# Moving eight more turned tiles of each batch from TensorE's barrier to GpSimd's mask, with a new slot table

## Time and profile before

| | |
|---|---|
| median of 3 runs | 874.0 us (873.55 to 875.01) |
| the profiled execution | 872.33 us |
| its span | 870.6 us |
| TensorE busy (matmul) | 94% |
| VectorE, ScalarE, GpSimd busy | 77%, 63%, 61% |

### The profile page before, as it was taken

The page is one execution under the profiler, slowest core; times in us unless marked ns, Lnnn a source line. Parts: engine busy times, 40 slices in busy tenths (PEclk is TensorE's granted clock), DMA queues, the critical chain, the costliest instruction groups (busy, mean ns, idle before and its releaser), DMA issues.

```text
span 870.6 us, 15444 instructions
## 1 busy us (share of the span) xinstructions
PE 814.5 (94%) x4860; PEld 467.4 (54%) x4860; DVE 674.6 (77%) x1950; ACT 544.3 (63%) x1230; POOL 532.0 (61%) x701
## 2 busy tenths in 40 slices
PE   3869899999999999999999999999999999999986
PEld 2223245646564655656565564656556565646466
DVE  5666669798887969788796978878797888878266
ACT  5427485765758485665848566574957657474832
POOL 4266766675857567585756658575665757474611
PEclk9899899999999999999999999999999999999999
DMA  3350505032140503113050402304050221300000
GB/s 94 100 138 3 141 1 141 1 102 53 43 111 1 152 2 114 41 58 96 5 148 2 141 13 78 76 22 132 2 153 2 85 69 36 106 2 13 13 1 25
DMA packets 49840, 54.75 MB, mean 63 GB/s; under 512 B 7264, under 2 KB 43616, under 8 KB 49760
## 3 DMA queue, kind: packets, MB, share of 16 engines
q1 hardware_dynamic: 49760, 53.76, 22.5%
HBM read 30.28 MB, written 23.07 MB: 61 GB/s over the span
## 4 chain that ended last, share of the span: by engine, by line
PE 54%; DVE 16%; POOL 11%; issue 7%; ACT 6%; DMA 3%; SPq 2%; POOLq 0%; DVEq 0%; ACTq 0%
PE adj L722 12%; PE pv L708 9%; PE score L680 7%; PE turned L694 7%; DVE scrap L955 6%; PE adj L717 6%; PE work L740 4%; PE turned L693 4%; POOL probs_t L547 3%; DVE adj_cos L974 3%; DVE adj_rbf L988 3%; DVE rbf_arg L983 2%; PE work L717 2%; POOL v_cos L632 2%; POOL v_cos L629 2%
## 5 line engine op out<-in xcount | busy, mean ns | idle before, releaser
L547 POOL TENSOR_TENSOR probs_t<-probs_t,keep_t 128x512 int32<-128x512 int32 x256 | 322.4, 1280 | 213.4 <-ACT probs_t L1126 213.1
L955 DVE CUSTOM_DVE_ANT_0 scrap<-score,mask_add 128x512 f32<-128x512 f32 x512 | 340.0, 683 | 67.6 <-PE score L680 65.3
L1126 ACT ACTIVATE probs_t<-turned 128x512 f32<-128x512 f32 x512 | 296.2, 601 | 110.5 <-PE turned L694 105.1
L680 PE MATMUL score<-qk_rows 96*128 96x512 bf16 x512 | 198.9, 388 | 12.1 <-DMA qk_rows<-k_dram 6.0
L694 PE MATMUL turned<-qk_rows 99*128 99x512 bf16 x512 | 196.2, 383 | 9.7 <-ACT probs_t L1126 8.8
L708 PE MATMUL pv<-probs_t,v_cols 128*32 128x512 f32 x1024 | 138.1, 612 | 0.0
L680 PEld LDWEIGHTS score<-qk_rows 96*128 96x128 bf16 x512 | 49.9, 98 | 119.8 <-DVE neg_max L955 55.2
L693 PE MATMUL turned<-bar_t,ident_b 128*128 128x512 bf16 x256 | 98.0, 383 | 0.7 <-ACT probs_t L1126 0.7
L694 PEld LDWEIGHTS turned<-qk_rows 99*128 99x128 bf16 x512 | 50.6, 99 | 54.7 <-ACT probs_t L1126 18.3
L1160 ACT ACTIVATE rbf_exp<-rbf_arg,rbf_bias 128x512 f32<-128x512 f32 x64 | 46.2, 722 | 34.7 <-DVE rbf_arg L983 32.8
L722 PEld LDWEIGHTS adj<-v_cos,adj_cos 128*128 128x128 f32 x480 | 62.8, 191 | 8.8 <-DVE out_sb L1011 0.6
(11 more groups left out here) (159 smaller groups left out, 1221.9 us busy)
## 6 DMA issues: line engine op xcount, KB each, us to landing
q_dram<-split SPq DMA_DIRECT2D x96, 128.0 KB
qk_rows<-q_dram SPq DMA_DIRECT2D x32, 384.0 KB, 4.3
k_dram<-split SPq DMA_DIRECT2D x48, 128.0 KB
qk_rows<-k_dram SPq DMA_DIRECT2D x32, 192.0 KB, 4.8
x_sb<-in_x_dram SPq DMA_DIRECT2D x16, 256.0 KB, 4.2
qk_rows<-k_dram SPq DMA_DIRECT2D x32, 128.0 KB, 4.9
out_dram<-out_sb SPq DMA_DIRECT2D x15, 256.0 KB, 2.5
qk_rows<-k_dram SPq DMA_DIRECT2D x32, 64.0 KB, 5.2
```

The source lines that it names most:

```text
L547: pool.tensor_tensor(tile, tile, keep_t[:, w // HG % T, :], ALU.mult).then_inc(probs_masked.sem, 1)
L680: pe.matmul(score_bank[u % 2][:, :], qk_rows[0:ROWS, b % 2, 0, h, t * P:(t + 1) * P], qk_rows[0:ROWS, b % 2, 1, h, :], start=True, stop=Tr ...
L955: dve.tensor_tensor_reduce(scrap[:, u % 2, :], score_bank[u % 2][:, :], mask_add[:, u % T, :], -1.0, 3.0e38, ALU.add, ALU.min, neg_max[:, ...
L1126: act.activation(probs_t[:, k % 4, w % HG, :], turned_bank[w % 2][:, :], ACT.Exp, scale=SCALE).then_inc(probs_ready.sem, 1)
```

## The change

`MASK_BY_PE` goes from `(2, 3)` to `(3,)`: 8 instead of 16 of a batch's turned tiles get the barrier, and GpSimd masks 24 instead of 16. Stages of all engines get new slots; `AT_BEFORE_LAST` and `AT_LAST` stay as they are. Nothing else is touched.

```diff
-MASK_BY_PE = (2, 3)
+MASK_BY_PE = (3,)
...
-    "hT": (-26,), "q": (-24,), "k": (-22,), "v": (-13,), "max_turn": (17, 32),
-    "pv": (28, 32, 36, 40, 44, 48, 52, 56), "y": (54, 59), "yT": (60,), "attn": (62,), "h2T": (66,),
-    "z": (69, 71, 72, 73), "zgT": (76,), "col": (78,), "zlT": (79,), "rbf": (79, 83, 85, 87),
-    "cos": (81, 83, 84, 90), "mix_cos": (92, 95, 96, 97), "mix_rbf": (94, 95, 96, 97),
+    "hT": (-26,), "q": (-24,), "k": (-22,), "v": (-12,), "max_turn": (18, 32),
+    "pv": (28, 32, 36, 40, 44, 48, 52, 56), "y": (53, 59), "yT": (61,), "attn": (62,), "h2T": (66,),
+    "z": (69, 71, 72, 73), "zgT": (76,), "col": (78,), "zlT": (79,), "rbf": (78, 83, 85, 87),
+    "cos": (81, 83, 84, 89), "mix_cos": (92, 95, 96, 97), "mix_rbf": (94, 95, 96, 98),
...
-    "ln_scale": (-28,), "hT_copy": (-26,), "q_hi": (-24,), "k_hi": (-22,), "max_copy": (17, 31),
-    "pv_copy": (42, 56), "yT_copy": (60,), "ln2_scale": (64,), "h2T_hi": (66,), "z_copy": (70, 71, 72, 74),
-    "z_sums": (71, 72, 74, 75), "zgT_hi": (75,), "col_copy": (77,), "zlT_hi": (79,), "rbf_exp": (82, 83, 86, 90),
+    "ln_scale": (-28,), "hT_copy": (-26,), "q_hi": (-24,), "k_hi": (-22,), "max_copy": (18, 32),
+    "pv_copy": (42, 56), "yT_copy": (61,), "ln2_scale": (64,), "h2T_hi": (66,), "z_copy": (70, 71, 72, 74),
+    "z_sums": (71, 72, 74, 75), "zgT_hi": (75,), "col_copy": (78,), "zlT_hi": (79,), "rbf_exp": (80, 83, 87, 89),
...
-    "ln_moments": (-36,), "hT_split": (-26,), "q_rest": (-24,), "k_rest": (-21,), "v_add": (-13,),
+    "ln_moments": (-35,), "hT_split": (-26,), "q_rest": (-24,), "k_rest": (-21,), "v_add": (-12,),
...
-    "zgT_lo": (76,), "zlT_lo": (79,), "rbf_read": (80, 83, 85, 87), "cos_read": (81, 83, 85, 90),
+    "zgT_lo": (76,), "zlT_lo": (79,), "rbf_read": (78, 83, 85, 88), "cos_read": (81, 83, 87, 90),
...
-    "ln_rstd": (-32,), "q_split": (-20,), "k_split": (-12,), "x_biased": (-13,), "ln2_rstd": (62,),
+    "ln_rstd": (-31,), "q_split": (-23,), "k_split": (-9,), "x_biased": (-14,), "ln2_rstd": (62,),
...
-    "qk_store": (-12,), "rows": (-6, -4), "x_next": (-9,), "max_load": (-2, 29), "store": (95,),
+    "qk_store": (-28,), "rows": (-8, -5), "x_next": (-24,), "max_load": (1, 25), "store": (99,),
```

## The result

The changed kernel takes 868.8 us (median of 20 runs, 864.87 to 874.08) against 874.25 (20 runs, 871.2 to 875.36): ratio 0.9941, 95% interval 0.9928 to 0.9955. It is 5.5 us faster, where 14.8 was forecast. Its runs spread over 9 us, those before over 4. The profiled execution took 870.53 us, 1.7 over its median.

What follows compares the result with a forecast made beforehand. TensorE was taken to bound batches 2 to 14; 13 x (1.72 - 0.15 - 0.35) = 15.9 us, with + 0.4 - 1.5, gave 14.8 us less: 859.2 us against the median. Forecast case 853 to 866; 8-in-10 range 846 to 873.

Steps and rivals of the forecast that it cites:

- The sign and the reason of the start: Batches 0 and 1: k_split comes four masks later, so the next batch starts later; 1.5 us taken as loss.
- rival A: Each batch's first score waits for its rows behind k_split, stores and loads; slower, up to 887 us; chance 0.13.
- 1.22 us: Gain per batch in batches 2 to 14: 1.72 of barriers less 0.15 and 0.35 of new stalls.
- B: Half the gain: a partly late row, attend or col costs 0.5 to 1.1 us a batch; 866 to 873; chance 0.19.
- a sum of six terms: Chain from GpSimd's queue through k_split, stores and loads to the next first score: 47.3 to 48.7 against 48.9 wanted.
- the wait of slot 14: TensorE's 0.56 us wait for ScalarE's exponential moves to the first rbf, about 0.7 us, growing by 0.15.
- VectorE's stretch: Second half of a batch: VectorE does not get faster with TensorE, 0.35 us of new stall, bounds 0 and 1.2.
- 0.93 + 0.5: TensorE's idle time per batch before, 0.93 us, plus the new stalls forecast, 0.15 and 0.35.
- C: All of the gain: TensorE never waits more than before; 841 to 853 us; chance 0.14.
- ScalarE's backlog: Moving max_copy to slot 32 takes 2 us of backlog from ScalarE before slot 8; costed at nothing.
- D: The change doesn't do what it says, the chosen tiles not going to GpSimd; ruled out.

Runs made afterwards that it cites:

- experiment 3: Changed kernel with k_split earlier, at slot 20 in place of 23: 864.23 us, ratio 0.9883.
- experiment 11: Changed kernel with q stores and q load first, fourth z_sums one slot later and k_split at slot 22: 862.77 us, ratio 0.9864.
- Experiment 12: Changed kernel with the load of the next x put ahead of the nine stores from the second batch on: 867.52 us, ratio 0.9918.
- experiment 4: Changed kernel with k_split one mask later, at slot 25 in place of 23: 892.93 us, ratio 1.0212.
- experiment 5: Changed kernel with SyncE's q stores ahead of its k stores and the q rows loaded before the wait for k: 862.07 us, ratio 0.9856.
- experiment 9: The changed kernel measured again, unaltered: 868.44 us, ratio 0.9927.
- experiment 10: Changed kernel with q stores and q load first and the fourth z_sums one slot later, k_split at slot 23: 859.57 us, ratio 0.9844.
- experiment 1: Kernel before with only the masks changed (GpSimd masks 24 tiles), all stages at the old slots: 899.57 us, ratio 1.0297.
- experiment 8: Kernel before with the masks changed and only q_split moved, to slot 9 from 12: 877.4 us, ratio 1.004.

## Why the prediction went wrong

**What held.** Eight barriers are worth 1.72 us of TensorE's work. GpSimd was forecast at 43.1 us a batch plus contention, it has 44.3 (531.83 / 12). The gapless run of its queue was right: start 16.3 after the first score (16.1 forecast), `k_split` ends at 40.6, 0.2 above the upper bound (39.0 to 40.4). All three meetings with L988 ahead of `k_split` cost the upper bound: L615 1.73 for 1.27, four masks 5.47 for 5.02, L577 1.09 for 0.62, together 1.38 us. On VectorE L988 grew from 4.2 to 4.85 us a batch, 0.6 (0.5 taken). That the two exclude each other is read off these coincidences and off the third L988, which followed `k_split` about in experiments 3 and 11; no run took the second SBUF input away. The sign and the reason of the start were right too: batch 1 is 2.7 us longer.

**The step that failed** is the end of rival A, where the prediction takes 3.0 us for the landing and 5.2 for the loads, "half a microsecond off for the second half; then the score comes at 47.3 to 48.7, in time." The first term was right (3.1 on average). The loads took 5.9 (5.95 and 5.77 in the two profiles). I took half a microsecond off 5.7 because the second half of the rows no longer follows at once. But before, with the second half right behind, the first half took 5.8 on average: so there was nothing to be had there. Experiment 12 says the same of the load of x: put elsewhere, it left the whole of store and loads at 8.92 us. With 5.9 and a `k_split` at 40.6 the score comes at 49.6. Its late batches put `k_split` at 40.74 in the mean of the first profile, and the score at 49.8. Rival A was the right mechanism at a fraction of its price: it did not make the kernel slower, for one batch takes 49.6 to 49.85 and not the 50.14 of before, but it took 0.7 to 0.9 of the 1.22 us. I had given it 0.13, and B, "a partly late row", 0.19. B's text and its 866 to 873 us are what came out.

Summed over the profiles (872.33 before, 870.53 and 869.13 after), the terms are:

| | forecast | first profile | second |
|---|---|---|---|
| up to batch 2's first score | +1.5 | +3.8 | +3.7 |
| batches 2 to 14 | -15.9 | -6.1 | -7.4 |
| batch 15 and the end | -0.4 | +0.5 | +0.5 |

So 8.5 to 9.8 of the missing microseconds lie in the batches that the rows pace. The start cost 2.3 more than taken: batch 1 began 1.1 us later and lasted 2.7 us longer, against 1.5 in all. The end lost half a microsecond where 0.4 was to be gained. No run separates the causes of these two.

Experiments 3, 4 and 5 show the chain from three sides: 1.4 us later costs 1.36 us a batch, 1.1 us shorter at the end gives 6.4 to 6.7 us in all, and where the rows are in time the batch takes 48.95.

**The reserve was counted wrongly.** I compared a sum of six terms, each with a margin, with a target 0.2 to 1.6 us away, and called it in time. The landing varies by itself, from 8.4 to 10.2 us behind the last store in one execution. In the changed kernel even the mean was too late, and the earliest landing still ended its batch at 49.04, so here the variation was not what cost the time. In experiment 5, where the rows land 0.5 us ahead of the score in the mean, it does cost: the three batches with late ones take 49.2 to 49.6, and no early one shortens one below TensorE's own 48.95. That may also be why the runs spread over 9 us (5 in experiment 9), against 0.8 and 2.4 in experiments 5 and 10. But in experiment 11 they spread over 4.6 with the rows in time, so it is not shown.

**The stalls.** A batch with the rows in time takes 48.95 us where 48.92 was forecast, but the stalls in it are not those of the forecast. I had the wait of slot 14 move to the first `rbf` and grow to 0.7. It stayed ahead of L694 at 0.78: ScalarE's queue holds back the exponential, and the `rbf` behind it finds its operand ready. The prediction's rows give 7.9 us from q's start to the end of `zgT_lo`, not 8.0, which decides nothing here. The 0.33 us ahead of `zlT` was not in the sum. I read it as the new order: `col` stands behind `rbf`, so `col_copy` is late for the bank that `zlT` writes. No run moved it back alone, but experiments 1 and 8, with the old order, have no such wait. And the 0.35 us I left for VectorE's stretch is not there in the changed kernel, but comes as 0.4 to 0.5 as soon as `k_split` goes earlier. 0.78 + 0.33 is 1.11 us of listed stalls against the 0.93 + 0.5 forecast.

**The other rivals.** C would have needed ScalarE's backlog to count; `max_copy` at slot 32 did end the wait of 4.80 us ahead of it, and TensorE had nothing of it. D is out: 128 L693 in place of 256.

**Open.** Why the fourth `z_sums` one slot later gives 5 us while the rows still bind in nearly every batch. The stall it shortens is not on that chain. Its profile has shorter landings (8.61 us, standard deviation of the loads 0.23 against 0.47 and 0.33), which may be the cause or one execution's chance. In experiment 4 the lower clock accounts for some 3.4 us of the profiled run of 890.96 (6.8 us at half the clock, an estimate), at a mean granted clock of 0.984. The other three runs had 0.978 to 0.982 and took 1.4 to 3.4 us more, so the clock may well be most of what lies above the range; their stretches at the lower clock are not seen.

## What to carry to other kernels

When work moves onto an engine with an in-order queue, look for what that queue feeds through DMA: here a split, three stores, four loads. Such a tail has no overlap with itself, so its reserve is the first thing to measure, first from the mean landing, which was already late here, and then from the latest. Move the suspected step both ways: here only the later one showed the full price, since the earlier one ran into the next bound. And a slot table fits one balance of work; half of this change alone was 25 us slower.

## What the runs showed of the hardware

- The four loads of the first half of the rows, 768 KB, had all landed 5.7 to 5.9 us after the first was issued (means of twelve batches: 5.66 in experiment 12, 5.83 before, 5.95 and 5.77 after), whether or not 256 KB went out just ahead of them or 768 KB behind them. The load that waits for the stores left 3.1 us after the last 128 KB store's issue with two others late beside it, and 4.4 us after it as the last of nine in a row.
- TensorE's granted clock fell from 2.4 to 1.2 GHz for some 3 us (once 6.8) in the midst of batches in which TensorE was busy for 93% of the time, behind 0.78 and 1.39 us of idle time close together (experiment 1, six batches of twelve; in the other six, with the same two idle times, it stayed full). With 0.78 and 0.34 in the same places it did not fall in any of the twelve (experiment 8). In experiment 4 it fell for 6.8 us, once, near the end of a 2.60 us wait.
- L988, a VectorE instruction with two SBUF inputs, took 0.68 us with GpSimd idle and up to 1.8 us with GpSimd busy (1.1 us more), and ended some 0.5 us after a GpSimd instruction did. The GpSimd instruction behind the seam took 0.45 us longer (1.73 for 1.27, 1.09 for 0.62). An L988 that starts in the seam keeps its 0.67 us, and GpSimd pays even so: the L577 beside it takes 1.09 for 0.61. In experiment 3, where that L577 meets no L988, it takes 0.61.
